# An audio tower with a mixture of experts: a reordered token stage, and the first expert fetches issued one block earlier

## The reference, cut to what matters

```python
def reference(x, h0, Wk, Wr, Wo, time_decay, time_first, router_w, router_b, W1, b1, W2, b2):
    h = tok(x, h0)                       # x: 32 x 750 x 256; two levels of an 8-tap filter, stride 2 -> 32 x 192 x 256
    h = h + attn(_layernorm(h), ...)     # k = x@Wk.T, r = v = x@Wr.T, a stable WKV scan over the 192 steps,
                                         # sigmoid(r) * y, @ Wo.T
    h = h + ffn(_layernorm(h), ...)      # 8 experts, top 2 of 8 by router logits, softmax over the two,
    return h                             # expert: relu(x@W1+b1)@W2+b2, 256 -> 1024 -> 256
```

## Time and profile before

| what | us |
|---|---|
| median of 3 runs (lowest to highest) | 1123.95 (1120.25 to 1124.64) |
| the profiled execution's own time | 1119.51 |
| its span, first to last instruction | 1117.4 |
| PE busy | 947.9 (85%) |
| DVE busy | 819.9 (73%) |
| ACT busy | 618.0 (55%) |
| POOL busy | 516.2 (46%) |
| mean granted PE clock, share of full | 0.913 |

### The profile page before, as it was taken

How to read it: one execution, slowest core, us unless ns; L and a number is a source line. 1 busy time by engine, 2 the same in 40 slices (tenths; PEclk the granted TensorE clock), 3 DMA queues, 4 the chain that set the end, 5 groups by cost and what they waited for, 6 DMA issues and landing times. The chain is left out here.

```text
span 1117.4 us, 19101 instructions
## 1 busy us (share of the span) xinstructions
PE 947.9 (85%) x5742; PEld 791.6 (71%) x5742; DVE 819.9 (73%) x2076; ACT 618.0 (55%) x1150; POOL 516.2 (46%) x462
## 2 busy tenths in 40 slices
PE   6787788778885531999999999999999999999994
PEld 4454555445553421899899899899899899899894
DVE  2678887888877862778778778778778778778762
ACT  2766777667766512456456456456456456456441
POOL 1003443224422354257557557557557557547524
PEclk9888879887987655999999999999999999999997
DMA  9223443334211144356456456456456456456413
GB/s 295 68 85 93 126 109 97 87 100 135 89 43 29 43 43 175 118 154 168 134 147 176 132 147 173 132 146 174 132 146 174 132 148 172 134 153 168 133 25 38
DMA packets 72695, 138.98 MB, mean 124 GB/s; under 512 B 11949, under 2 KB 63790, under 8 KB 68682
## 3 DMA queue, kind: packets, MB, share of 16 engines
q0 software_dynamic: 31136, 98.34, 33.3%
q1 hardware_dynamic: 41514, 40.08, 12.8%
HBM read 110.52 MB, written 27.86 MB: 124 GB/s over the span
## 5 line engine op out<-in xcount | busy, mean ns | idle before, releaser
L1092 ACT ACTIVATE hid<-hp,b 128x512 f32<-128x512 f32 (+1 forms) x248 | 158.5, 639 | 302.8 <-PE hp L1127 295.0
L1139 PE MATMUL acc<-whi,hhi 128*128 128x256 f32 x880 | 245.9, 279 | 0.0
L1139 PE MATMUL acc<-whi,hlo 128*128 128x256 f32 x880 | 245.9, 279 | 0.0
L1139 PE MATMUL acc<-wlo,hhi 128*128 128x256 f32 x880 | 245.3, 279 | 0.0
L1223 DVE CAST hhi<-hid 128x512 fp32r<-128x512 f32 (+1 forms) x248 | 106.9, 431 | 148.4 <-ACT hid L1092 147.7
L1054 POOL DMA_INDIRECT out_rows<-yout,dest x110 | 180.0, 1636 | 63.7 <-issue 52.0
L1127 PE MATMUL hp<-xhi,whi 128*128 128x512 f32 (+1 forms) x496 | 187.8, 379 | 10.0 <-DVE xlo L1170 7.6
L1127 PE MATMUL hp<-xlo,whi 128*128 128x512 f32 (+1 forms) x496 | 184.0, 371 | 0.0
L1127 PE MATMUL hp<-xhi,wlo 128*128 128x512 f32 (+1 forms) x496 | 183.8, 371 | 0.0
L1139 PEld LDWEIGHTS acc<-wlo,hhi 128*128 128x128 f32 x880 | 165.3, 188 | 9.0
L1068 ACT ACTIVATE whi<-raw 128x512 fp32r<-128x512 f32 x248 | 154.3, 624 | 31.5 <-DMA raw<-in_ew,idx 31.5
(11 more groups left out here) (187 smaller groups left out, 1463.4 us busy)
## 6 DMA issues: line engine op xcount, KB each, us to landing
xin<-in_x SPq DMA_DIRECT2D x32, 512.0 KB
xin<-in_x SPq DMA_DIRECT2D x32, 256.0 KB
token_rows<-xs SPq DMA_DIRECT2D x16, 259.0 KB, 2.6
out_rows<-h SPq DMA_DIRECT2D x16, 256.0 KB, 2.5
token_rows<-xs SPq DMA_DIRECT2D x32, 64.8 KB, 2.4
out_rows<-h SPq DMA_DIRECT2D x32, 64.0 KB, 2.1
xg<-token_rows,tid POOLq DMA_INDIRECT x110, 2.9
out_rows<-yout,dest POOLq DMA_INDIRECT x110, 4.0
```

Source lines behind the costliest of these rows:

```text
L1092: act.activation(hid[:, c % 2, 0:j.r * P], hp[c % 2][:, 0:j.r * P], ACT.Relu, bias=b1[:, j.s, c:c + 1]).then_inc(hid_done, 1)
L1139: last = pe.matmul(acc_of(j, r), h_[:, c % 4, r * P:(r + 1) * P], w_[:, j.s, at:at + C], start=c == 0 and n == 0 and r % 2 == 0, stop=c == ...
```

## The change

In the first block, the order within the bodies changes.

- ACT: the copy of `conv_ps` to `h` (p0) moves up from behind `kr(0)` to stand right behind the `dist` activations. `ed` moves ahead of `kr(0)`. `kr(0)` and `kr(1)` follow one another. The root of p0's statistics moves from behind the Ln of `div` to right behind `kr(1)`, ahead of p3's root. Ln and Exp of `div` work in place (no `lnd`).
- PE: `kr(p1, 3)` moves ahead of the transposes of `xs`, so the four projections follow one another.
- DVE: p0's statistics move from behind `div` up to behind `t2`, ahead of `h1`, with up to two router steps behind each statistics instruction and each aggregate; p0's `shift` moves up to behind p3's. `gate_sum` (which waits for `ed`) comes after `e2sv` instead of between p3's statistics.
- The convolution's input buffer `xin` becomes a view of `tables.raw`, the experts' weight buffer, which exists in both blocks.

At the end of the first block DVE copies the indices of tiles 0 and 1, and POOL issues four indirect DMAs that stood in the second block: the weights of tiles 0 and 1 first, then, when every list scatter has landed, the token numbers of tiles 0 and 1. The first block's end no longer drains POOL (`no_gpsimd_drain=True`). The second block begins on POOL with `gather_x` of tile 0.

```diff
+        self.raw = sb("raw", [P, 2, WROW])
+        self.idx, self.tid = sb("idx", [P, 4, 3], U32), sb("tile_tid", [P, 2, R], U32)
...
+class Fetch:
...
+    def weights(self, j):
+        t = self.tables
+        self.pool.indirect_dma_start(t.raw[:, j.s, :], None, self.ew, bass.IndirectOffsetOnAxis(t.idx[:, j.i, 0:1], 0)).then_inc(t.w_in[j.s], 16)
+
+    def tokens(self, j):
+        t = self.tables
+        self.pool.indirect_dma_start(t.tid[:, j.s, 0:j.r], None, self.groups[j.r],
+                                     bass.IndirectOffsetOnAxis(t.idx[:, j.i, 1:2], 0)).then_inc(t.tid_in[j.s], 16)
...
+def indices(dve, tables, j):
+    dve.tensor_copy(tables.idx[:, j.i, :].unsqueeze(1), tables.table[:, bass.ds(j.col, 1), :]).then_inc(tables.idx_ready, 1)
...
-        xin = sb("xin", [P, 2, 2, NKI, C])
+        assert 4 * NKI * C <= 2 * WROW
+        xin = tables.raw[:, :, :].rearrange("p a n -> p (a n)")[:, 0:4 * NKI * C].rearrange("p (s b n c) -> p s b n c", s=2, b=2, n=NKI)
...
-        block = ctx.enter_context(nc.Block())
+        block = ctx.enter_context(nc.Block(no_gpsimd_drain=True))
...
             rounds(pool, body)
 
+            fetch, t0 = Fetch(pool, tables, ew, lists), Tile(0, 0)
+            pool.wait_ge(tables.idx_ready, 2)
+            fetch.weights(t0)
+            fetch.weights(t0.nxt())
+            for s in range(2):
+                pool.wait_ge(listed[s], 96 * (PAIRS // 2))
+            pool.sem_inc(slots_seen, 1)
+            fetch.tokens(t0)
+            fetch.tokens(t0.nxt())
...
+                if p0:
+                    act.wait_ge(conv_done, p0.at(1, 1))
+                    act.sem_inc(act_seen, 1)
+                    act.activation(h[:, bass.ds(p0.at(3), 3), :], conv_ps[:, 0:3 * C].rearrange("p (t c) -> p t c", c=C),
+                                   ACT.Copy).then_inc(h_taken, 1)
                 if p1:
                     act.wait_ge(kr_done, p1.at(4))
...
+                if p1:
+                    kr(0)
+                    kr(1)
+                if p0:
+                    root(p0, ln1, N_LN1, 6, mv1[:, :, 1], lv1, rs1, rstd1)
                 if p3:
                     root(p3, ln2, N_LN2, 7, mv2[:, :, 1], lv2, rs2, rstd2)
...
-                    for j in range(3):
+                    for j in range(4):
                         kr(p1, j)
...
-                if p1:
-                    kr(p1, 3)
...
+                if p0:
+                    dve.wait_ge(h_taken, p0.at(1, 1))
+                    statistics(p0, lambda t: tile_of_h(p0, t), st1, mv1, ln1, N_LN1, 0, lambda: route_to(min(14, routed[0] + 2)))
                 route_to(14)
...
-                    route_on()
-                    statistics(p3, lambda t: h1[:, p3.s, t, :], st2, mv2, ln2, N_LN2, 1, route_on)
+                    route_to(15)
+                    statistics(p3, lambda t: h1[:, p3.s, t, :], st2, mv2, ln2, N_LN2, 1, lambda: route_to(16))
...
                     shift(p3, mv2, rs2, nb2, rstd2, xn2_ready, ln2)
+                if p0:
+                    shift(p0, mv1, rs1, nb1, rstd1, xn_ready, ln1)
                 route_to(19)
...
             def first():
-                pool.wait_ge(idx_ready, 1)
-                gather_tid(T0)
-                gather_w(T0)
                 gather_x(T0)
-                pool.wait_ge(idx_ready, 2)
-                gather_tid(T0.nxt())
                 gather_b2(T0)
-                gather_w(T0.nxt())
                 gather_x(T0.nxt())
```

More of the change, by code:

```diff
@@ L119, in __init__, with sem @@
         self.ident = sb("ident", [P, P])
+        self.raw = sb("raw", [P, 2, WROW])
+        self.idx, self.tid = sb("idx", [P, 4, 3], U32), sb("tile_tid", [P, 2, R], U32)
+        def sem(name):
+            return ctx.enter_context(nc.semaphore(name))
+        self.idx_ready = sem("idx_ready")
+        self.w_in, self.tid_in = [sem("w_in0"), sem("w_in1")], [sem("tid_in0"), sem("tid_in1")]
+class Fetch:
+    def __init__(self, pool, tables, ew, lists):
+        self.pool, self.tables, self.ew = pool, tables, ew
+        self.groups = {n: lists.rearrange("(g r) a -> g (r a)", r=n) for n in (R, RH)}
+    def weights(self, j):
[7 more added lines that the diff above has]
+    dve.tensor_copy(tables.idx[:, j.i, :].unsqueeze(1), tables.table[:, bass.ds(j.col, 1), :]).then_inc(tables.idx_ready, 1)
 def rounds(eng, body, until=PAIRS):
@@ L136, in rounds, with tokens_to_experts @@
         body(*pairs(i))
-def tokens_to_experts(nc, x, taps, taps_down, wkT, wrT, woT, decay, first, rw, rb, out, rows, lists, tables):
+def tokens_to_experts(nc, x, taps, taps_down, wkT, wrT, woT, decay, first, rw, rb, ew, out, rows, lists, tables):
     ctx = ExitStack()
@@ L426, in body @@
                     act.wait_ge(state, p2.at(N_STATE, 5))
[L427 to L430, removed]
+                    act.activation(div[:, :, :], div[:, :, :], ACT.Ln).then_inc(inv_ready, 1)
                     act.wait_ge(inv_ready, p2.at(2, 1))
                     act.wait_ge(o_ready, p2.at(N_OUT))
-                    act.activation(inv[:, :, :], lnd[:, :, :], ACT.Exp, scale=-1.0).then_inc(inv_ready, 1)
+                    act.activation(inv[:, :, :], div[:, :, :], ACT.Exp, scale=-1.0).then_inc(inv_ready, 1)
             rounds(act, body)
@@ L590, in statistics @@
                     dve.bn_aggr(mv[:, t, :], st[:, t, :]).then_inc(done, 1)
+                    step()
             def shift(q, mv, rs, nb, roots, used, done):
@@ L955, in experts @@
     with ctx:
-        idx = sb("idx", [P, 4, 3], U32)
-        raw = sb("raw", [P, 2, WROW])
+        raw, idx, tid = tables.raw, tables.idx, tables.tid
         whi, wlo = sb("whi", [P, 2, B1AT], F32R), sb("wlo", [P, 2, B1AT], F32R)
         b1, b2s = sb("b1", [P, 2, FC]), sb("b2s", [P, 2, C])
-        tid = sb("tid2", [P, 2, R], U32)
         xg = sb("xg", [P, 2, R, ROW])
@@ L972, in experts @@
         xt = [ps("xt0"), ps("xt1")]
[L974 to L975 removed]
+        idx_ready, w_in, tid_in, waits_over = tables.idx_ready, tables.w_in, tables.tid_in, sem("waits_over")
+        x_in, b2_in, y_sent = ([sem(f"{n}{s}") for s in range(2)] for n in ("x_in", "b2_in", "y_sent"))
         xt_done, xhi_done, xlo_done = sem("xt_done"), sem("xhi_done"), sem("xlo_done")
@@ L991, in _ @@
         def _(pool):
-            groups = {n: lists.rearrange("(g r) a -> g (r a)", r=n) for n in (R, RH)}
+            fetch = Fetch(pool, tables, ew, lists)
             def end_of_waits():
                 pool.sem_inc(waits_over, 1)
-            def gather_w(j):
-                pool.indirect_dma_start(raw[:, j.s, :], None, ew, bass.IndirectOffsetOnAxis(idx[:, j.i, 0:1], 0)).then_inc(w_in[j.s], 16)
-            def gather_tid(j):
-                pool.indirect_dma_start(tid[:, j.s, 0:j.r], None, groups[j.r],
-                                        bass.IndirectOffsetOnAxis(idx[:, j.i, 1:2], 0)).then_inc(tid_in[j.s], 16)
             def gather_x(j):
@@ L1034, in body @@
                     end_of_waits()
-                    gather_w(a)
-                    gather_tid(a)
+                    fetch.weights(a)
+                    fetch.tokens(a)
                 if p.exists():
@@ L1258, in audio_tower @@
         tables = Tables(nc, ctx)
-        tokens_to_experts(nc, x, taps, taps_down, wkT, wrT, woT, decay, first, rw, rb, out, rows, lists, tables)
+        tokens_to_experts(nc, x, taps, taps_down, wkT, wrT, woT, decay, first, rw, rb, ew, out, rows, lists, tables)
         experts(nc, ew, b2, out, rows, lists, tables)
```

25 lines of the change are left out of this document (4 added, 21 removed).

## The result

The changed kernel takes **1103.75 us** (median of 4 runs, 1099.68 to 1105.3) against 1123.12 (4 runs, 1120.25 to 1124.64): ratio 0.9824, 95% interval 0.9804 to 0.9844. The forecast was 1092 in a range of 1082 to 1107. The sign and the range held, but 19.4 us were gained where 31 were forecast, and the likeliest case's own range (1086 to 1099) did not hold. The profiled execution took 1102.31, its span is 1100.2, so the span fell by 17.2. Of the experiments further down, runs 2 and 3 have one slow execution each (1180.61 and 5156.47 us), which their ratios leave out, while the time given is the median of all four.

The account below looks back on a forecast made before the run. PE fills the experts' block, so time follows its first `up`, behind token rounds set by a cross-engine chain. 1119.51 - 31.3 + 2 = 1090.2, plus half of the 4.4 median offset: 1092 us, range 1082 to 1107.

Parts of the forecast that it names:

- the likeliest case: Whole kernel: the prediction's own forecast of 1092 us, own range 1086 to 1099, chance 0.66.
- The round: Token stage, twelve middle rounds: 22.97 us each falls to 20.9, saving 2.07 a round, 24.8 in all.
- The price of `ranks` ahead of `kr(0)`: PE in the round: `kr(0)` stands behind `ranks`, which waits for the later `sel`, so it starts 1.6 us later.
- The rounds before 70.58: Token stage's early rounds: they gain by the same moves, 5.5 us in all (3 to 7).
- the last ones: Token stage's last rounds: both orders the same but for one round, gain 1 us (0 to 3).
- The token stage: All 20 rounds up to the end of `table`: 24.8 + 5.5 + 1 = 31.3 us earlier.
- PE's clock: Rival: projections at 1.2 GHz make rounds 23.0 or more, total 1117 us; in half of the rounds 1105; chance 0.15.
- The handover: End of `table` to first `up`, 24.04 us before: 25.95, so 2 longer, as `tid` waits behind both tiles' weights.
- weights of tile 0 issued at 0.8, landed at 9.3 (8.5): Handover, counted from the end of `table`: tile 0's weights land 8.5 us after their issue.
- The second tile's weights: Handover: tile 1's weights land 5.5 us after tile 0's, at 14.8 behind `table` (4.8 to 6.5).
- The drain: POOL at the first block's end: without it the barrier falls some 1 us earlier, but removal is worth nothing by itself.
- The experts' block: From the first `up` on: nothing altered behind its first tile, it only starts earlier or later, 0 us.

Follow-up runs that it names:

- run 2: Kernel before with only the changed memory placement (shared `raw`, `idx`, lists' tile, `xin` as view, Ln in place), no instruction moved: 1153.22 us, ratio 1.0112 to before.
- run 3: Kernel before with everything of the change but the order: early fetches, shared memory, no drain: 1157.21 us, ratio 1.0154 to before.
- run 5: Changed kernel with PE's rank matmuls moved behind the first two projections, ahead of the other two: 1119.01 us, ratio 0.9816 to before.
- run 12: Kernel before with the new order and Ln in place, but `kr(3)` left behind the `x2` transposes, old memory and handover: 1110.61 us, ratio 0.9901 to before.
- run 4: Changed kernel, first block fetching tile 0's token numbers then its weights after the list scatters land, tile 1's fetches in the second block: 1119.78 us, ratio 0.9835 to before.
- run 11: Changed kernel with only tile 0's weights fetched in the first block, tile 1's in the second behind tile 0's bias: 1097.13 us, ratio 0.9780 to before.
- run 8: Changed kernel as it is, measured again on another, slower chip: 1126.61 us, ratio 0.9885 to before on that chip.
- run 9: Changed kernel with GpSimd's drain at the end of the first block kept: 1107.05 us, ratio 0.9869 to before.
- run 7: Kernel before with only the token lists' tile declared ahead of `whi`, shifting `whi`, `wlo`, `b1`, `b2s` by 32 bytes: 1150.12 us, ratio 1.0086 to before.
- run 6: Changed kernel with two unused 32-byte tiles, so `whi` and `wlo` start at a multiple of 64 again: 1113.88 us, ratio 0.9770 to before.
- run 1: Kernel before with the token stage's new order and Ln in place alone; memory, handover and drain as before: 1112.51 us, ratio 0.9757 to before.
- run 10: Changed kernel with the three edits of run 4, run 5 and run 6 together: 1083.45 us, ratio 0.9652 to before.

## Why the prediction was right in its sign and 12 us off in its size

- **The bound** was read rightly: the experts' block is filled by PE, the round is a chain over three engines, and the time follows the first `up`.
- **The round**: walked to 20.9, measured 21.07; each station came within 0.35 us of the walk (`sel` ends 9.4 against 9.73, `kr(0)` 9.8 against 10.01, the `kr(1)` copy 12.65 against 12.86, `nb` 14.1 against 14.23). The waits came too: 0.92 for `h` (0.7) and less for the root (0.34 for 1.2). The error starts at `sel` and is passed on. Twelve rounds gave 22.7 for 24.8. The price of `ranks` ahead of `kr(0)` is real: run 5 took it away, and the round fell by 0.57, not by the whole 1.6. That others bind then is argued, not shown.
- **The rounds before 70.58** gave 5.57 (5.5 forecast), the last ones 0.9 (1). The token stage: 29.2 of 31.3.
- **PE's clock**, the rival with 0.15, did not come: the clock of a round rose. Its idle before the transposes went from 3.23 to 0.93 us. The Trainium skill ("TensorE: Matmul & The Clock Gate", HAM oscillation) ties a fall to half rate to long idle stretches, and the trace agrees in direction. But run 5 lost clock with a shorter round still (0.90 to 0.83), so fewer idle microseconds in all are no promise. And in run 12, with `kr(3)` in its old place, a loss of this rival's kind did come, by the convolution and not by the projections: five of the twelve rounds ran at half clock for their first 6 us and were 2.3 us longer.
- **The handover** is the first step that failed, by its size. The mechanism, token lists held by the weights ahead of them, is shown by runs 4 and 11 (5 us for each 2.1 MB ahead). The term that was wrong is "weights of tile 0 issued at 0.8, landed at 9.3 (8.5)": they landed 14.8 behind the table, since they in turn stood behind the last list scatters. In place of 8.5 it took 14.3. The second tile's weights came 4.9 later (17.9 from issue, the maximum above; 5.5 forecast), and everything after it as walked, so 5 us late. I had the scatters' landing (423.5 of before, 4.2 behind the table) in hand and applied the queue's rule to `tid` alone, not to the weights. That the scatters are what holds the weights is shown by run 4, where the weights are issued behind their landing and take 8.5. Full DMA engines are not the reason (share 0.32). The size has a second part: the scatters themselves landed later than in the trace that I walked from, 6.9 behind the table for 4.2. SP's wait for them, as in the earlier trace rows, in the kernel after and in run 5, where the table ends at 385.36:

```profile
L338 SPq EVENT_SEMAPHORE  x1: 28/28/28, 397.0 to 397.0; - x1
L338 SPq EVENT_SEMAPHORE  x1: 28/28/28, 389.8 to 389.8; - x1
```

With the same fetches, run 5 has the landing at 4.4 and a handover of 27.7, run 3 has 5.0 and 28.0, run 8 has 5.4 and 29.1, the first result 6.9 and 31.0. So with a landing as early as before, some 2 of the 5 us would be left to the weights' wait, and some 3 come with the later landing (an estimate from these four executions, on three chips). Why it differs between executions, no run shows.
- **The drain** was called worth nothing. Kept, it costs some 3.6 us (run 9; 3.3 between the medians), as it ends behind `tid`. I had taken its end from the trace of before, where it begins 7 us ahead of the table's end (412.2 against 419.3); behind the new fetches it begins 9.5 us after it (403.6 against 394.15).
- **The experts' block** was assumed unchanged. That is the second step that failed, and the prediction had no term for it: "the change alters nothing in it behind its first tile". It alters where `whi` and `wlo` lie: 50816 before, 50848 after, by 32 bytes for the lists' tile that now stands ahead of them. Run 7 shows that this alone slows the kernel before, run 6 that undoing it alone speeds the kernel after; runs 1 to 3 agree. It costs 5 us in the first result and on chip A (from the parts above; on chip A the block takes 673.4 and 673.1 in runs 10 and 12 with the tiles at a multiple of 64, and 679.0 and 678.2 in runs 9 and 11 without), and 10 to 14 in the times on chips B and C.

Sum of the misses: 2.1 + 5.0 + 5.0 = 12.1, and 1102.3 less 1090.2 is 12.1.

**To carry to other kernels.** When a fetch is moved earlier in a shared queue, list everything that is still in flight ahead of it and everything that will stand behind it; the small transfer on the critical path goes first, the large one that has slack after it, and an early issue behind an unfinished transfer buys nothing. When tiles are declared in another place, compare the address of each operand of the inner loop modulo 64 before and after, and try a pad if it moved. And in a round that no engine fills, look at the single rounds before naming a wait as the cost: the longest wait here (3.45) stood in rounds that lost nothing by it, and what `kr(3)` cost in its old place was a late convolution in about every other round. Moving it gave more than half of the round's gain.

## What the runs showed of the hardware

- A matmul whose moving operand (`whi`, `wlo`: 256 columns of 4 bytes) starts 32 bytes past a multiple of 64 has a median of 281 ns (282 in one group) instead of 279 to 280; the `up` matmuls, where the same tiles are the loaded weights, don't get longer (391 to 394). Seen in 13 kernels with no exception; two addresses were tried at 0 and one at 32, no others.
- GpSimd's drain at the end of the block took 15.26 us in the kernel before and 15.37 in run 9, where 4.2 MB of weights were in flight: its length did not follow what was landing. In runs 1, 2, 7 and 12, which have it too, it took 15.6, 15.2, 15.8 and 17.1.
- The same kernel differs by 1.6 to 2.1% between chips (1122 and 1140 us for before, 1104 and 1127 for the kernel after). Stretches of half clock, in a block in which PE is nearly always busy, make part of it (14 to 38 us on two chips, 0 on chip A), and they were longer with the shifted address.
- In run 12 a slow `kr(3)` (2.2 to 2.7 us for 1.46, at a granted clock of 0.68 to 0.79) was followed each time by a round with a lower clock at its start (0.50 or 0.73 over its first 6 us) that took 1.3 to 2.3 us longer.
